# The first layer norm's tile turned by VectorE and two DRAM transfers instead of by TensorE

## The reference

```python
# A: windowed self attention (16 heads of 16, windows of 128 tokens, rolled by 64)
h = _ln(x) * (1 + sc_msa) + sh_msa
h = _self_attn(h, w_qkv, b_qkv, w_so, b_so);      x = x + h * g_msa
# B: cross attention to 77 context rows, with the 16 largest scores of each row kept
h = _ln(x) * (1 + sc_mca) + sh_mca
h = _topk_cross_attn(h, context, w_q, b_q, w_kv, b_kv, w_co, b_co);  x = x + h * g_mca
# C: gated MLP, hidden width 1024
h = _ln(x) * (1 + sc_mlp) + sh_mlp
h = _swiglu(h, w_m1, b_m1, w_m2, b_m2);           x = x + h * g_mlp
# D: cross attention with a plain softmax
xq = _ada_ln(x_q, t_vec, Wss_q, bss_q)
...
return x_q + (out @ Wp + bp)
```

## Time and profile before

| | |
|---|---|
| median of 3 runs | 1042.06 us (1039.88 to 1044.54) |
| the profiled execution | 1043.68 us |
| its span in the trace | 1041.9 us |
| busy share: PE, PEld | 94%, 83% |
| busy share: DVE, ACT, POOL | 80%, 75%, 68% |
| mean granted TensorE clock | 0.971 of full speed |
| DMA | 23.14 MB, mean 22 GB/s |

### The profile page before, as it was taken

How to read it: one execution, slowest core, us unless ns; L and a number is a source line. 1 busy time by engine, 2 the same in 40 slices (tenths; PEclk the granted TensorE clock), 3 DMA queues, 4 the chain that set the end, 5 groups by cost and what they waited for, 6 DMA issues and landing times.

```text
span 1041.9 us, 33051 instructions
## 1 busy us (share of the span) xinstructions
PE 983.6 (94%) x10980; PEld 868.1 (83%) x10980; DVE 834.8 (80%) x4234; ACT 782.9 (75%) x1681; POOL 705.4 (68%) x1100
## 2 busy tenths in 40 slices
PE   6885699999999999999999999999999999999985
PEld 5563588898888898889988888988999888888874
DVE  2356789989888888889898888888898988888631
ACT  1143478888888888888888888888888888888662
POOL 2257355777777778777777777787777777767754
PEclk9788699999999999999999999999999999999996
DMA  8305000000000000000000000000000000000000
GB/s 294 42 27 125 32 7 8 7 12 13 13 13 11 4 12 12 13 13 12 12 12 12 13 10 4 13 12 12 13 13 12 12 12 8 7 8 7 7 6 16
DMA packets 33848, 23.14 MB, mean 22 GB/s; under 512 B 22979, under 2 KB 31427, under 8 KB 33168
## 3 DMA queue, kind: packets, MB, share of 16 engines
q1 hardware_dynamic: 33680, 21.02, 7.8%
HBM read 16.19 MB, written 4.83 MB: 20 GB/s over the span
## 4 chain that ended last, share of the span: by engine, by line
PE 87%; issue 3%; DMA 3%; DVE 3%; SPq 2%; ACT 2%; POOL 2%; POOLq 0%; DVEq 0%; ACTq 0%
PE ps L1242 21%; PE ps L1251 10%; PE ps L1123 9%; PE ps L1231 8%; PE ps L1220 7%; PE ps L1204 7%; PE ps L1195 4%; PE ps L1154 3%; PE ps L1171 3%; PE ps L1184 3%; PE ps L1112 2%; PE ps L1134 2%; PE ps L1144 2%; DMA w_mod_sb<-in_w_mod 1%; PE ps L1053 1%
## 5 line engine op out<-in xcount | busy, mean ns | idle before, releaser
L1242 PE MATMUL ps<-hT_C,w_m_sb 128*128 128x128 f32 x2048 | 250.7, 275 | 0.2 <-DVE hidden_C L934 0.2
L1242 PEld LDWEIGHTS ps<-hT_C,w_m_sb 128*128 128x128 f32 x2048 | 241.6, 192 | 2.7 <-issue 0.7
L678 ACT ACTIVATE silu_C<-ps,cols_sb 128x128 f32<-128x128 f32 x256 | 90.7, 367 | 72.9 <-PE ps L1242 72.0
L503 POOL TENSOR_TENSOR p_D<-scores_D,rc_D 128x616 f32<-128x616 f32 x64 | 78.2, 1225 | 79.1 <-DVE rc_D L905 79.1
L503 POOL TENSOR_TENSOR p_B<-p_B,rc_B 128x616 f32<-128x616 f32 x64 | 77.8, 1217 | 67.4 <-DVE p_B L891 66.1
L1251 PE MATMUL ps<-w_m_sb,hidden_C 128*128 128x256 f32 x512 | 121.0, 379 | 0.0
L934 DVE SCALAR_TENSOR_TENSOR hidden_C<-ps,cols_sb,silu_C 128x128 f32<-128x128 f32 x256 | 87.9, 344 | 33.4 <-ACT silu_C L678 33.0
L883 DVE MATCH_REPLACE8 scores_left_B<-mx_B,scores_left_B 128x77 f32<-128x77 f32 x512 | 108.3, 223 | 0.0
L879 DVE MATCH_REPLACE8 scores_left_B<-mx_B,scores_B 128x77 f32<-128x77 f32 x512 | 108.1, 222 | 0.2 <-issue 0.2
L1251 PEld LDWEIGHTS ps<-w_m_sb,hidden_C 128*128 128x128 f32 x512 | 94.6, 190 | 11.4
L833 DVE TENSOR_REDUCE mx_A<-ps 128x8 f32<-128x1024 f32 x64 | 75.4, 1221 | 26.8 <-PE ps L1154 26.6
(11 more groups left out here) (180 smaller groups left out, 2574.6 us busy)
## 6 DMA issues: line engine op xcount, KB each, us to landing
x_A<-in_x SPq DMA_DIRECT2D x64, 64.0 KB, 2.2
out<-y_D SPq DMA_DIRECT2D x64, 64.0 KB, 2.1
w_mod_sb<-in_w_mod SPq DMA_DIRECT2D x2, 1024.0 KB, 11.9
w_m_sb<-in_w_m SPq DMA_DIRECT2D x1, 2048.0 KB, 7.6
w_m_sb<-in_w_m SPq DMA_DIRECT2D x1, 1024.0 KB, 10.0
w_qkv_sb<-in_w_qkv SPq DMA_DIRECT2D x1, 768.0 KB, 5.8
w_gate_sb<-in_w_gate SPq DMA_DIRECT2D x1, 768.0 KB, 7.5
rows_sb<-in_rows SPq DMA_DIRECT2D x1, 768.0 KB, 8.8
```

Of the source, the lines that this page charges most:

```text
L503: g.tensor_tensor(where, src, rc, ALU.mult).then_inc(n_ok[s], 1)
L678: sc.activation(SA[:, j, :], bank(f"C.up{j}")[:, 0:P], ACT.Silu, bias=col("bm1_a", j)).then_inc(sa_ok, 1)
L1242: ins = mm(bank(f"C.up{j}")[:, half * P:(half + 1) * P], w_m1[:, k, m:m + P], HT["C"][:, t % HT_COPIES["C"], k, :], start=(k == 0), stop=( ...
```

## The change

For tiles 1 to 31 of stage A (`TURNED = 1`) PE's transposes are left out. DVE turns each 32x32 block of `XN["A"]` in place of the whole (`turn_input`), SP writes the blocks to DRAM in four transfers, one for each band of 32 tokens, in runs of 128 bytes, waits until they have landed, and reads the tile back with one transfer whose rows are 1 KB long (`move_input`); `modulate` then reads `XT` in SBUF instead of the PSUM bank. Tile 0 goes the old way. `normalise` of A waits for the turn of the tile before, and no longer for PE.

```diff
+TURNED = 1
...
+        turned = nc.dram_tensor("xn_turned", [2, ROWS, QUAD, KC, ROWS, QUAD], F32, kind="Internal").ap()
...
+        XB = sb("xn_blocks_A", [P, CH])
+        XT = sb("xn_turned_A", [P, KC, P])
...
+            def move_input(t):
+                n = t - TURNED
+                sp.wait_ge(xb_ok, n + 1)
+                for i in range(ROWS):
+                    sp.dma_start(turned[t % 2, :, :, :, i, :].rearrange("j k c q -> k c j q"),
+                                 XB[quad(i), :].rearrange("k (c j q) -> k c j q", c=KC, j=ROWS)).then_inc(xb_out, 16)
+                sp.wait_ge(xb_out, 16 * ROWS * (n + 1))
+                sp.wait_ge(h_ok["A"], t)
+                sp.dma_start(XT[:], turned[t % 2].rearrange("j k c i q -> (j k) c (i q)")).then_inc(xt_in, 16)
...
+            def move_later_input(t):
+                if t >= TURNED:
+                    move_input(t)
...                                             # SP's body
                 run(load_next_x, i, 0)
                 run(store_y, i, 9)
+                run(move_later_input, i, 1)
                 if starts(i, 2):
                     set_up_flat("B")
...
             def normalise(t, s):
                 act.wait_ge(rstd[s], 4 * t + 4)
-                if not first(t):
+                if s == "A" and t > TURNED:
+                    act.wait_ge(xb_ok, t - TURNED)
+                elif not first(t):
                     act.wait_ge(h_ps[s], t)
...
             def modulate(t, s):
-                act.wait_ge(h_ps[s], t + 1)
+                from_turned = s == "A" and t >= TURNED
+                if from_turned:
+                    act.wait_ge(xt_in, 16 * (t - TURNED + 1))
+                else:
+                    act.wait_ge(h_ps[s], t + 1)
...
                 for c in range(KC):
-                    ins = sc.activation(HT[s][:, t % HT_COPIES[s], c, :], bank(f"{s}.th")[:, c * P:(c + 1) * P], ACT.Identity,
+                    src = XT[:, c, :] if from_turned else bank(f"{s}.th")[:, c * P:(c + 1) * P]
+                    ins = sc.activation(HT[s][:, t % HT_COPIES[s], c, :], src, ACT.Identity,
...
+            def turn_input(t):
+                if t < TURNED:
+                    return
+                n = t - TURNED
+                dve.wait_ge(xn_ok["A"], t + 1)
+                if n:
+                    dve.wait_ge(xb_out, 16 * ROWS * n)
+                v.transpose(XB[:], XN["A"][:]).then_inc(xb_ok, 1)
...                                             # DVE's body
                 run(residual, i, 8, "D")
+                run(turn_input, i, 1)
                 run(statistics, i, 0, "A")
...
+            def transpose_first_h(t):
+                if t < TURNED:
+                    transpose_h(t, "A")
...                                             # PE's body
-                run(transpose_h, i, 0, "A")
+                run(transpose_first_h, i, 0)
```

More of the change, by code:

```diff
@@ L222, in block_kernel @@
         u_ps, sa_ok, g_ok = sem("u_ps"), sem("sa_ok"), sem("g_ok")
+        xb_ok, xb_out, xt_in = sem("xb_ok"), sem("xb_out"), sem("xt_in")
         tmp_ok, yd_ok, y_out = sem("tmp_ok"), sem("yd_ok"), sem("y_out")
```

## The result

The changed kernel takes 1046.12 us (median of 18 runs, 1042.29 to 1050.22), the kernel before 1041.64 us beside it (18 runs, 1039.22 to 1044.54). The ratio is 1.0046, with a 95% interval of 1.0034 to 1.0057: slower by 4.5 us (the difference of the medians) where 6.4 us less was forecast.

The account below looks back on a forecast made before the run. PE was taken to bound the bodies. Savings of 5.9 us in 27 bodies, 0.2 for tile 4 and 0.56 for tile 1 made 6.7, less 0.3: 6.4 us off 1042.06, said as 1036 us, range 1030 to 1045.

Parts of the forecast that it names:

- Added to DVE: DVE's turn of 0.43 us ahead of the statistics and `qmax_A` in each body: price 0, with 0.93 us left before `scores_t`.
- eaten on the way: Rival: DVE's 0.43 us makes `hidden` or `qmax_A` late in each body; 1039 to 1048 us, likeliest 1040 to 1043; chance 0.18.
- The pair's price per body: Two PE transposes removed per tile save 0.22 us in each of 27 bodies, 5.9 us.
- That the delay is caught up at `hidden` 3: DVE's 0.43 us delay ends at `hidden` 3, where DVE idled 0.54 us; nothing carries into the next body.
- The start, tile 1's pair: Removing tile 1's two PE transposes, taken to run at the lower clock in the start, saves 0.56 us.
- The start, tile 2's pair: Removing tile 2's two PE transposes in the start saves 0, since PE soon waits for ACT and DVE anyway.
- The trip through DRAM: SP's four writes and read back take 6 to 9 us, at least 3.3 us before `modulate` needs the tile: price 0.
- too late: Rival: the tile returns after `modulate` of A wants it, delaying ACT's fixed order; up to 1063 us; chance 0.10.
- the strided one: Rival: SP's strided writes to DRAM take 19 times a plain transfer, giving 1550 us; chance 0.01.
- ACT from SBUF: `modulate` reading SBUF instead of PSUM costs 0.07 us more per instruction, 0.13 taken for two; 0 on the path.
- SP's queue and the load of `x`: Loads and stores queued behind the new transfers on SP, including the start's load of `x`, are not delayed: 0.
- Tile 4's stall: In the start, tile 4's turn stands ahead of a `qmax_A` PE already awaited 0.17 us: 0.3 us given back.

Follow-up runs that it names:

- the banks exchanged: Changed kernel with the PSUM banks of stage B's first and second transpose groups swapped (`B.PT0` on 6, `B.PT1` on 5): 1037.87 us, ratio 0.9959.
- two instructions more or less: Kernel before without PE's stage A transposes, turn or transfers: 1040.64 us; the same with PE transposing tile 2 again: 1037.1 us.
- the transfers alone: Kernel before with SP's five transfers per tile added, tile not turned, nothing removed, nobody waiting for the read: 1041.67 us, ratio 1.0001.
- from tile 5 on: Changed kernel with `B.PT0` and `B.PT1` on swapped banks and `TURNED = 5`, so PE transposes tiles 0 to 4: 1034.65 us, ratio 0.9943.

## Why the prediction was wrong

The direction was wrong. The step that failed is "Added to DVE", price 0: `qmax_A` had 0.14 us of slack at its first user and not 0.93, and PE stands 0.28 to 0.33 us for it in every body. The rival "eaten on the way" had this mechanism, at 0.18. Its outer figures, 1039 to 1048, hold the result, though partly by luck: its likeliest, 1040 to 1043, do not, and half of the 4.5 us lie outside the bodies that it speaks of. Point by point:

- *The pair's price per body*, 0.22 us: right. Without it, and without any stall, a body is 28.37 to 28.42 us against 28.63; 28.40 was forecast. An estimate from the 390 ns (bf16) of the Trainium skill (VectorE: DVE Perf Modes, The three transpose paths) would be 0.78 us for two, which no run shows.
- *Added to DVE*: this is the step that failed. The operation was sized right (435 ns on average, 434 forecast), but the consumer was the wrong one. The prediction took `scores_t`, which reads `qmax_A`, and found 0.93 us of slack. PE's first user is the step ahead of it in PE's order, `transpose_p` of stage B, which waits for `qmax_A` only because its bank held what `qmax_A` reads. There the slack was 500.91 - (499.89 + 0.88) = 0.14 us in the body at 500, as the kernel before's timeline has it:

```profile
499.89 0.88 DVE L843 SCALAR_TENSOR_TENSOR qmax_A<-ps,mask_sb,qT_A 128x256 f32<-128x256 f32 x2
500.91 1.28 PE L1204 MATMUL ps<-ident_sb,p_B 128*128 128x128 f32 x10
```

  The evidence stood among the prediction's own rows: PE waiting 0.17 us for `qmax_A` at `ps<-ident_sb,p_B` at 133.85, which it priced as a single event of the start. In the changed kernel such a wait comes in all bodies, 0.28 us in the one shown and 0.3 by the lengths of the bodies, more than the 0.22 that the change brings.
- *That the delay is caught up at `hidden` 3*: right, since with the banks exchanged and the turn in its place no wait of PE is left; but of no use in the changed kernel, where PE had stood already.
- *The start, tile 1's pair*, 0.56 us of gain: wrong. From the start of `w_mod`'s products to that of the context's keys it takes 48.95 - 46.58 = 2.37 us before and 50.70 - 48.33 = 2.37 after. PE cannot go on there before DVE's `shiftT`; without the pair it stands 0.42 us for that, and with it the pair fills the time. The pair did not run at the lower clock either, as the prediction has it: the granted clock was 1.00 from 48.40 to 48.95.

```profile
48.33 1.95 PE L1079 MATMUL ps<-scT,w_mod_sb 128*128 128x4 f32 x16 [0.30 <-DVE gate L817]
50.70 2.31 PE L1105 MATMUL ps<-ctxT_sb,w_kv_B_sb 128*128 128x308 f32 x8 [0.42 <-DVE shiftT L807]
```

- *The start, tile 2's pair*, 0: wrong, and by more than its own length. It filled time in which PE would have stood, and its price is below nothing. Shown are the 2 us (two instructions more or less), that the stretch at the lower clock lasts 6.8 us with the pair and 10.2 without, and that this sets the length of the products, whose end starts the transfers that the rest of the start waits for. That the 2 us come through this path alone is the reading of the profiles, not an experiment of its own; and why so little work on PE moves the clock stays open. The rows of the prediction do not show the clock in the start.
- *The trip through DRAM*: right, at the lower of its bounds. Four writes with four dimensions took 2.58 us to issue (2.3 to 3.1 forecast), SP waited 2.2 us for them on average (69.0 us in 31), and the tile came back after 6.1 us where 12.4 were allowed. The largest unknown cost nothing, and the rival that rests on it, "too late" at 0.10, had no part in the result. The same holds of the strided one.
- *ACT from SBUF*: 482 ns against 456 for one instruction (medians), where the nearest forms had given 0.07 more; hidden, as said.
- *SP's queue and the load of `x`*: right, by the transfers alone (ratio 1.0001).
- *Tile 4's stall*, 0.3 us given back once: the one place where the sum had this wait, and the sum took it 1 time instead of some 27.
- *The sum*, 6.4 us: near what a kernel gives in which both faults are mended, 1041.5 - 1034.65 = 6.9 us from tile 5 on (5.9 by the ratio). In part that is luck, since the exchange of banks may bring 1.3 of them, and of the sum only 27 x 0.22 = 5.9 belongs to tiles 5 to 31.

So the 4.5 us are 2.2 from the body (a stall of 0.3 against a gain of 0.2, 27 times) and 2.3 outside it, which go away when PE transposes tiles 1 and 2 again (3.2 us by the ratios, 1.3 to 5). Without the two faults the change is worth having: the version with the banks exchanged and `TURNED = 5` beats both kernels.

## What to carry to other kernels

When an operation is put ahead of another on an engine with time to spare, its price is not read from that engine's idle time but from the slack of everything behind it, and the first to wait for it may be a step that never touches the result and only wants the buffer that it frees: look through the claims on each PSUM bank, and take any wait of 0.1 or 0.2 us of the bound engine for the named tile as a sign that the slack is already spent. A step is worth removing from the bound engine only where that engine is bound; in a start where it stands and runs at its lower clock, the removed work can have been free, or better than free. And turning a tile through DRAM in runs of 128 bytes cost nothing here but 6 us of delay, on a queue and on DMA engines that had little else to do (4% busy in a body before, 10% with it).

## What was not expected of the hardware

The length of a stretch at the lower clock moved with very little work. In the eight profiles with the pair of tile 2, which takes 0.69 us there and leaves PE standing 0.26 or 0.59 us before the products, the granted clock stayed at 1.2 GHz for 6.8 us and rose to 2.4 between 78.5 and 80.9 us of the span; in the four without, where PE stood 0.88 us, it stayed there for 10.2 us and rose between 83.0 and 85.0. The Trainium skill (TensorE: Matmul & The Clock Gate, Part 1: The HAM clock gate) says that the penalty of this ramp varies from run to run and is under 1% of a typical span. The 2 us of 1042 here, 0.2%, agree, but they are nearly half of what the change does in all.
